# TensorE's order within a unit of two attentions: maxima, scores, scores, maxima, values instead of scores, maxima, scores, values, maxima

## The reference

```python
x = x + attn_a(_layernorm(x), Wq, Wc, Wk, Wv, Wo)     # 32 heads of 16, rotary, no mask
x = x + ffn(_layernorm(x), lora_A, lora_B, W, bias, lora_weights)
x = x + attn_b(_layernorm(x), w_attn, b_attn, w_proj, b_proj)  # 32 heads of 16, ALiBi, causal
x = x + ffn(_layernorm(x), ...)

# attention, both kinds: softmax over the 1024 keys
scores = einsum('bqhd,bkhd->bhqk', q, k) * scale      # b adds slope * (k - q), and -inf above the diagonal
out = einsum('bhqk,bkhd->bqhd', softmax(scores), v).reshape(B, S, 512) @ Wo
```

## Time and profile before

| | us |
|---|---|
| median of 3 runs | 2026.8 (2019.76, 2026.8, 2048.18) |
| the profiled execution's own time | 2042.08 |
| its span in the profile | 2040.3 |
| attention a, first to last scores and values | 209 to 1023 |
| attention b, the same | 1347 to 1902 |
| PE / DVE / ACT busy over the span | 1685.3 / 1395.5 / 986.5 |

### The profile page before, as it was taken

The page is one execution under the profiler, slowest core; times in us unless marked ns, Lnnn a source line. Parts: engine busy times, 40 slices in busy tenths (PEclk is TensorE's granted clock), DMA queues, the critical chain, the costliest instruction groups (busy, mean ns, idle before and its releaser), DMA issues. The chain is left out here.

```text
span 2040.3 us, 28808 instructions
## 1 busy us (share of the span) xinstructions
PE 1685.3 (83%) x11228; PEld 773.5 (38%) x11228; DVE 1395.5 (68%) x2495; ACT 986.5 (48%) x1169; POOL 119.7 (6%) x218
## 2 busy tenths in 40 slices
PE   6994788888888888888879998778888888888698
PEld 4552222222222222222235676533333333333376
DVE  3767788886888888768547443367677767776376
ACT  3331566665666666657711111025556556566410
POOL 3231000000000000000001000010000000000100
PEclk9996799996999999869989998859799979999899
DMA  7677122223322222220151445732444435350331
GB/s 213 194 217 171 40 48 48 48 48 48 48 48 48 48 48 48 48 48 10 51 153 41 124 124 167 174 64 50 71 74 73 74 52 94 52 95 10 97 106 62
DMA packets 116840, 167.26 MB, mean 82 GB/s; under 512 B 20828, under 2 KB 58092, under 8 KB 116588
## 3 DMA queue, kind: packets, MB, share of 16 engines
q1 hardware_dynamic: 114880, 160.11, 35.0%
q0 software_dynamic: 1824, 5.31, 1.5%
HBM read 100.34 MB, written 64.50 MB: 81 GB/s over the span
## 5 line engine op out<-in xcount | busy, mean ns | idle before, releaser
L493 DVE TENSOR_REDUCE a_mxp<-a_ps_m 128x1 f32<-128x512 f32 x1024 | 657.9, 685 | 153.2 <-PE a_ps_m L378 152.9
L472 ACT ACTIVATE a_p<-a_ps_s 128x1024 f32<-128x1024 f32 x512 | 519.8, 1025 | 294.3 <-PE a_ps_s L418 291.3
L493 DVE TENSOR_REDUCE b_mxp<-b_ps_m 128x1 f32<-128x512 f32 (+3 forms) x768 | 387.6, 552 | 174.4 <-PE b_ps_m L378 167.0
L472 ACT ACTIVATE b_p<-b_ps_s 128x1024 f32<-128x1024 f32 (+3 forms) x384 | 309.2, 811 | 279.3 <-PE b_ps_s L418 275.1
L378 PE MATMUL a_ps_m<-a_slot_qk 48*128 48x512 f32 x640 | 165.7, 514 | 86.5 <-DVE a_mxp L493 86.4
L435 PE MATMUL a_ps_o<-a_p,a_slot_v 128*32 128x512 f32 x1280 | 184.2, 649 | 0.0
L378 PEld LDWEIGHTS a_ps_m<-a_slot_qk 48*128 48x128 f32 x640 | 62.2, 190 | 292.1 <-DVE a_mxp L493 281.5
L378 PE MATMUL a_ps_m<-slot_qk 48*128 48x512 f32 x384 | 110.8, 573 | 74.3 <-DVE a_mxp L493 62.3
L418 PE MATMUL a_ps_s<-a_slot_qk 50*128 50x512 f32 x640 | 137.0, 423 | 0.0
L354 PE MATMUL b_ps_m<-b_masks 64*128 64x64 bf16 x1024 | 63.9, 202 | 80.5 <-DVE b_mxp L493 72.5
L378 PEld LDWEIGHTS a_ps_m<-slot_qk 48*128 48x128 f32 x384 | 41.2, 210 | 205.1 <-DVE a_mxp L493 187.1
(11 more groups left out here) (162 smaller groups left out, 2073.6 us busy)
## 6 DMA issues: line engine op xcount, KB each, us to landing
va_groups<-w_o SPq DMA_DIRECT2D x16, 512.0 KB, 3.7
ka_parts<-pa_parts SPq DMA_DIRECT2D x16, 512.0 KB, 3.7
qa_parts<-pa_parts SPq DMA_DIRECT2D x32, 256.0 KB, 3.7
kb_parts<-slot_memory SPq DMA_DIRECT2D x16, 512.0 KB, 3.5
qb_parts<-slot_memory SPq DMA_DIRECT2D x32, 256.0 KB, 3.3
vb_groups<-w_proj SPq DMA_DIRECT2D x16, 512.0 KB, 3.7
a_slot_qk<-qa_parts SPq DMA_DIRECT2D x60, 128.0 KB, 4.5
a_slot_qk<-ka_parts SPq DMA_DIRECT2D x48, 128.0 KB, 6.9
```

What stands on the lines that cost most here:

```text
L472: act.activation(p_sb[:, (2 * u + pair) % NP, :, off:CHUNK], ps_s[:, 2 * pair:2 * pair + 2, off:CHUNK], ACT.Exp, scale=scale).then_inc(exp ...
L493: dve.tensor_reduce(to, from_, AX.X, ALU.max).then_inc(piece_taken, 1)
```

## The change

The two calls of `ahead` change places with the calls before them: the first part of the maxima is issued ahead of the unit's first scores, both pairs of scores follow one another, the second part of the maxima comes next, and the values of the unit before close the unit. Nothing is added, removed or resized, and no wait is changed; the waits move with their instructions. `cut`, the other engines' programs and the order of the maxima among themselves stay.

```diff
@@ def step(s, j), in the tensor block of attention()
                 for u in range(NU):
                     lo, hi = AHEAD + before_unit[u], AHEAD + before_unit[u + 1]
                     cut = lo + PAIR * ((hi - lo + PAIR) // (2 * PAIR))
+                    ahead(s, j, lo, cut)
                     scores(s, j, u, 0)
-                    ahead(s, j, lo, cut)
                     scores(s, j, u, 1)
+                    ahead(s, j, cut, hi)
                     if u:
                         values(s, j, u - 1)
-                    ahead(s, j, cut, hi)
                 values(s, j, NU - 1)
```

## The result

The changed kernel takes **1964.8 us** (median of 4 runs, 1959.67 to 1981.73) against 2028.0 for the kernel before on the same chip (4 runs, 2019.76 to 2048.18): a ratio of 0.969, with the interval 0.960 to 0.978. The forecast was 1978. The profiled execution took 1965.01, its span 1963.2. Ratios compare the fast runs of each kernel (one run of e6 took 3442 us and is left out), so they can differ a little from the quotient of two medians.

A forecast was written before the change was run, and what follows sets the result against it. A ring of waits between TensorE's maxima and VectorE's reductions was taken to set the pace. 2042 less 60 (old falls to half clock) less 66 (shorter groups) gave 1916, plus 16 x 4 gave 1980; forecast 1978, range 1955 to 2005.

The forecast's parts named there:

- The ring of a unit of a: Attention a's chain front maxima, middle maxima, values, next front maxima: 2.71 us a unit instead of 2.95.
- The step into the values: From middle maxima to values in a: 0.43 us by the trace, 0.33 by the tiling-mode rule alone; 0.43 taken.
- The moved wait: Second scores' wait for the previous unit's second exp, now ahead of middle maxima and values: slack 0.3 or more, no cost.
- The turned unit: Units of a with turned maxima, which now follow the middle pair: 3.34 us against 3.54, 0.20 saved.
- The end of a group: In a, last values wait for their own exp: 3.96 instead of 2.95; unit 0 then 2.56 instead of 2.94.
- The stretch without values: At a group's end in a, from last values' end to next values: 4.27 us instead of 3.49, light on TensorE.
- A group of b: One group of attention b at full clock: 32.3 us instead of 34.03, 1.8 saved, 27 us in all.
- The clock: Drops to half clock (falls) behind group ends in both attentions: about 16 of 30 ends, replacing 60 us of falls before.
- the price of 4: Cost of one drop to half clock in the new order: 4 us instead of 6.
- falls come at group ends: Half clock begins behind the light stretch without values at the groups' ends, in a and b.
- The gain goes into the clock: Rival: 20 to 25 drops to half clock at 5 us, kernel 2010 to 2040, within 2%; chance 0.32.
- Clock held: Rival: ten drops to half clock of 3 us or fewer, kernel 1925 to 1950; chance 0.18.

The follow-up runs named there:

- e6: Kernel before with the new order in attention b only, the old one kept in a: 2044.6 us (1.011).
- e7: Kernel before, old order kept, with a group's last values issued in unit 0 of the next group: 2032.0 us (1.003).
- e8: e4 with first scores computed twice more, unread, between the two opening pairs of maxima in units 0, 5, 6 and 8 of b: 1879.2 us (0.920).
- e3: Kernel before reordered to first maxima, first scores, second maxima, second scores, values; in a the old cycle begun at another call: 2274.2 us (1.118).
- e2: Kernel before with only the second maxima moved ahead of the values, first scores still opening the unit: 2244.2 us (1.110).
- e4: Changed kernel with a group's last values, their result copy and stores carried into unit 0 of the next group: 1910.9 us (0.944).
- e10: e4 run once more, unchanged, on the chip of e8: 1910.2 us (0.934).

## Why the prediction was right, and where its steps were off

**The ring of a unit of a: right.** 1.28 + 0.43 + 1.00 = 2.71, each term met to 0.01 us. The step into the values was the disputed one, 0.43 or 0.33. The Trainium skill, TensorEngine Tiling (Array Packing), section Tiling Modes, says that a change of tiling mode drains the TensorE and gives no time for it. The prediction read it as 0.33 for both steps; the new rows say 0.43, as the earlier trace rows did.

**The moved wait: right.** No wait for exps appeared in an ordinary unit at the full clock. VectorE's idle time in such a unit is 0.13, where 0.14 was predicted.

**The turned unit: too dear.** 3.34 was predicted, 3.15 measured. The prediction put 0.43 from the turned maxima to the values; the rows show the values starting 0.01 us behind the first of the two turning matmuls, and the second falling among them. Both are listed as 128*32, where maxima to values, 48*128 to 128*32, is the step of 0.43. Two such units at 0.19 are most of the 0.5 us by which a group of a came out shorter.

**The end of a group: right in kind.** Unit 15 was put at 3.96 and unit 0 at 2.56; from 533.72, the front maxima of unit 15, to 537.54 is 3.82, and from there to 540.11 is 2.57. The wait of the last values for their own exps, put at 1.01, is listed 16 times between 220 and 940, 14.8 us in all. The stretch without values is 4.28 for 4.27. A group of a is 45.18 for 45.7.

**A group of b: right**, 32.01 for 32.3. Together the groups at the full clock give 49 + 30 = 79 us where the sum had 66. These 13 us are about as much as the measured time lies under the forecast.

**The clock: the total right, the places wrong.** The prediction had about 16 falls, all at group ends, 4 us each, 64 us in all, spread over both attentions. Measured, a's price against the full clock is 17 us and b's 57, each with the half clock that the stage begins in: 74 in all, where before had 49 + 28 = 77. The prediction's own terms, with 15 us for the entries, were 64 + 15 = 79 after and 60 + 15 = 75 before. In a there are seven falls, as before, not more; each costs 1.2 or 2.3 us (46.38 and 47.48 against 45.18), because the stretches are 3.4 or 6.8 us long, where before they were up to 31 us. The step that failed here is the price of 4, taken too near to the old 6. In b there are 17 stretches where before had three, and they are not only at group ends. The step that failed is that "falls come at group ends". In a all seven do, 3.4 to 4.0 us behind ScalarE's copy. In b seven of the 17 do, 3.4 to 4.4 us behind it, and ten stand elsewhere. e7 and e8 show another such place in b, two pairs of maxima of a wide unit with nothing between them. The two errors had opposite signs, and the clock's total came out near the forecast's by that, which is luck.

**The rivals.** "The gain goes into the clock" is what happened in b, taken alone: e6, with b changed and a not, stands at 1.011. "Clock held" is what happened in a. The length of the unit alone is no guard: e3 kept it and lost the clock. The Trainium skill, TensorE: Matmul & The Clock Gate, Part 1, has the clock follow how busy TensorE has recently been. The falls in a agree, behind the lightest stretch of the group; e2's b, 93% busy at 0.50 for 686 us, does not if one reads "busy" as the profile's busy share, since the stretch of before that was 93% busy at 0.50 ended after 31 us. What of TensorE's work counts was not isolated.

**Open.** Why e2's b never comes back to the full clock for 686 us, while e4's comes back after 3.4. Why the clock falls at the bare pairs in e7 and e4 and not in the kernel before, which has such pairs too. What stands at the ten other places of b in the changed kernel itself: e8 was built on e4 alone.

## What to carry to other kernels

Write TensorE's order around the one pair that waits for a buffer: independent work between the two dependent instructions, and the long values directly behind them. Then look at the granted clock stage by stage before believing a sum of instruction lengths: two orders with the same unit length in a were 237 us apart here, and the longer group end explains 15 of them in a. Where the clock falls at fixed places of a loop, fill those places, by carrying work over the loop's end (the ratio went from 0.969 to 0.944) or even by work that nobody reads (31 us between e10 and e8), as long as it fits in a wait that is there anyway.

## What the runs showed of the hardware that was not expected

- The same cycle of instructions begun at another call (e3) changes the granted clock in a from 0.92 to 0.81. In b, where the two parts of the maxima change places as well, it goes from 0.93 to 0.63.
- TensorE can stay at half clock for 686 us while its instructions fill 93% of the time (e2); another stretch as full at half clock was over after 31 us (before).
- 240 matmul instructions whose results nobody reads made a stage of 511 us 28 us shorter (e10 to e8).
- A pair of matmuls is listed shorter behind another pair: the first maxima behind scores took 0.40 us for 0.50, and the step to the next maxima, which waits for their reduction, was 1.18 for 1.28 (e2).
